# One product for router logits and actor outputs, and two channel attentions in the opening of a four-layer kernel

## The reference

```
x = x + channel_attention(layernorm(x))      # A
x = x + mixture_ffn(layernorm(x))            # F, weights shared by both F layers
x = x + attention_sps(layernorm(x))          # B
x = x + mixture_ffn(layernorm(x))            # F
```

```
probs  = softmax(h @ router_w.T)                          # 8 experts
a_h    = gelu(h @ actor_w1.T + actor_b1)                  # 50 hidden units
k      = argmax(clip(a_h @ actor_w2.T + actor_b2)) + 1    # 6 outputs
mask   = rank(probs) < k                                  # the k best experts
out    = sum_e where(mask, probs, 0)[e] * down_e(silu(gate_e(h)) * up_e(h))
```

## Time and profile before

| | |
|---|---|
| three runs | 488.0, 489.6, 489.79 us, median 489.6 |
| the profiled execution | 489.73 us |
| its span (first to last instruction) | 487.9 us |
| TensorE, VectorE, ScalarE, GpSimd busy | 98%, 62%, 55%, 64% |
| mean granted TensorE clock | 0.997 |

### The profile page before, as it was taken

One profiled execution on the slowest core, in us unless ns is written; L12 is line 12 of the kernel. 1 busy time (PEld: TensorE's weight loads), 2 busy tenths in 40 slices (PEclk: granted clock), 3 DMA queues, 4 the chain that ended last, 5 costly groups with the idle time before them and its releaser, 6 DMA issues.

```text
span 487.9 us, 6499 instructions
## 1 busy us (share of the span) xinstructions
PE 476.1 (98%) x2039; PEld 342.7 (70%) x2039; DVE 303.0 (62%) x718; ACT 266.2 (55%) x484; POOL 312.4 (64%) x326
## 2 busy tenths in 40 slices
PE   8899899999999999999999999999999999999997
PEld 7777666677676666666676766677676777778886
DVE  3656342646487768499836884359754565666563
ACT  3395636646724693348742649235772456456551
POOL 5355789336948576486463466467675586778774
PEclk9999899999999999999999999999999999999999
DMA  7700000000000000000000000000000000000000
GB/s 240 247 0 2 0 1 0 1 1 1 1 0 2 1 0 1 1 1 1 0 1 0 1 2 0 1 1 5 19 0 2 0 23 1 0 1 10 15 0 22
DMA packets 7933, 7.36 MB, mean 15 GB/s; under 512 B 732, under 2 KB 7772, under 8 KB 7900
## 3 DMA queue, kind: packets, MB, share of 16 engines
q1 hardware_dynamic: 7900, 6.96, 4.4%
HBM read 5.91 MB, written 1.05 MB: 14 GB/s over the span
## 4 chain that ended last, share of the span: by engine, by line
PE 83%; ACT 2%; DVE 1%; POOL 1%; issue 0%; ACTq 0%; DVEq 0%; POOLq 0%
PE bank L1313 21%; PE bank L1128 17%; PE bank L1130 17%; PE bank L1129 17%; PE bank L1351 3%; PE bank L1249 1%; PE bank L1343 1%; PE bank L1151 1%; PE bank L1363 1%; PE bank L1321 1%; PE bank L1257 1%; PE bank L1291 1%; ACT L778 1%; PE bank L1239 0%; PE bank L1219 0%
## 5 line engine op out<-in xcount | busy, mean ns | idle before, releaser
L647 POOL TENSOR_TENSOR t<-t,sl 128x512 f32<-128x512 f32 x105 | 148.6, 1421 | 80.9 <-DVE t L1069 61.7
L778 ACT ACTIVATE sl<-bank 128x512 f32<-128x512 f32 x168 | 99.2, 596 | 126.3 <-PE bank L1130 114.5
L1313 PE MATMUL bank<-t,WD 128*128 128x512 f32 x256 | 126.0, 592 | 0.0
L1069 DVE TENSOR_TENSOR t<-bank,sbc 128x512 f32<-128x512 f32 x105 | 72.3, 689 | 72.2 <-PE bank L1130 70.5
L1128 PE MATMUL bank<-xhF,WGh 128*128 128x512 f32 x167 | 89.8, 538 | 1.0 <-ACT sl L778 0.9
L647 POOL TENSOR_TENSOR t<-t,sbc 128x512 f32<-128x512 f32 x63 | 79.4, 1288 | 0.2
L1069 DVE TENSOR_TENSOR t<-bank,sl 128x512 f32<-128x512 f32 x63 | 42.9, 686 | 55.8 <-ACT sl L778 30.0
L1128 PE MATMUL bank<-xhF,WUh 128*128 128x512 f32 x168 | 66.8, 397 | 1.1 <-DVE t L1069 1.1
L1130 PE MATMUL bank<-xhF,WUl 128*128 128x512 f32 x168 | 66.3, 395 | 0.0
L1129 PE MATMUL bank<-xlF,WUh 128*128 128x512 f32 x168 | 66.3, 394 | 0.0
L1130 PE MATMUL bank<-xhF,WGl 128*128 128x512 f32 x167 | 66.2, 397 | 0.0
(11 more groups left out here) (210 smaller groups left out, 722.9 us busy)
## 6 DMA issues: line engine op xcount, KB each, us to landing
stage<-in_gate SPq DMA_DIRECT2D x7, 192.0 KB, 5.7
stage<-in_up SPq DMA_DIRECT2D x7, 192.0 KB, 5.7
WD<-in_down SPq DMA_DIRECT2D x7, 192.0 KB, 5.7
X<-in_x SPq DMA_DIRECT2D x4, 256.0 KB, 5.4
out<-X SPq DMA_DIRECT2D x3, 256.0 KB, 2.3
raw<-in_small SPq DMA_DIRECT2D x1, 384.0 KB, 4.2
out<-X SPq DMA_DIRECT2D x2, 128.0 KB, 1.9
raw<-in_small SPq DMA_DIRECT2D x1, 192.0 KB, 2.7
```

What stands on the lines that cost most here:

```text
L647: pool.tensor_tensor(t2[k % NT2][:, :], t2[k % NT2][:, :], by[:, :], ALU.mult).then_inc(a_done, 1)
L778: act.activation(sl[k % NSL][:, :], bank[k % 2][:, :], ACT.Silu).then_inc(silu_done, 1)
L1069: dve.tensor_tensor(t2[k % NT2][:, :], bank[2 + k % 2][:, :], by[:, :], ALU.mult).then_inc(t2_done, 1)
L1313: r = pe.matmul(OACC[:, :], WD[:, c, :], t2[k % NT2][:, :], start=(c == 0), stop=(c == CH - 1 or k == TAIL[0] - 1))
```

## The change

Router: the second weight `w2` becomes 72 x 14: the actor's 50 x 6 and, at rows 64 to 71, an 8 x 8 identity in columns 6 to 13. "gelu" writes into rows 0 to 49 of `xa`, and "act" multiplies all 72 rows of `xa` by it, which gives actor outputs and router logits per token in one bank. The transposes of "rt" on TensorE and their turn are gone; the VectorE steps "rt", "rcmp", "rrank", "rmax" stand behind "act", and its bank is freed by "actk". The step lists of the feed-forwards follow, and that of the second starts earlier.

Opening: both of the first two batches go through channel attention in it, and `A1_STEPS` is gone. For these two, the raw tokens are transposed; the weights take up the norm weight and the centring (a product with a centred, scaled identity, "wn"); the Gram matrix is the raw tokens times tokens over variance, with a VectorE reciprocal for GpSimd's power; and the root is put on when "y" is added. Batch 0 needs no "am2": its values are made ahead ("vT"). Sums of squares are a step of their own ("asq"). An early idle Silu loads its table. The warming products are fewer and read zeros. SP loads the columns and batch 1 earlier, and waits for `w2`'s constants before `w2`. The head mask takes three GpSimd instructions.

```diff
-PRELUDE = [("stats", "A", 0), ("rstd", "A", 0), ("warm", 0), ("xn", "A", 0), ("ag", 0), ("xT", "A", 0), ("ar", 0), ("wph", 0), ("wph", 1),
-           ("warm", 1), ("asim", 0), ("ass", 0), ("apow", 0), ("wpl", 0), ("swh", 0), ("wv", 0), ("warm", 2), ("ascale", 0), ("asT", 0),
-           ("amax", 0), ("warm", 3), ("aexp", 0), ("awo", 0), ("am", 0), ("stats", "A", 1), ("rstd", "A", 1), ("wpl", 1), ("am2", 0),
-           ("y", 0), ("warm", 4), ("wp", 3), ("stats", "F", 0), ("rstd", "F", 0), ("xn", "A", 1), ("ag", 1), ("xn", "F", 0), ("wp", 4),
-           ("xT", "F", 0), ("xT", "A", 1), ("xl", "F", 0), ("ar", 1), ("swl", 0)]
-WARM = (12, 2, 4, 7, 10)
+PRELUDE = [("warm", 0), ("xT", "A", 0), ("warm", 1), ("stats", "A", 0), ("rstd", "A", 0), ("wn", 0), ("xn", "A", 0), ("ag", 0),
+           ("stats", "A", 1), ("rstd", "A", 1), ("xn", "A", 1), ("ar", 0), ("ag", 1), ("asq", 0), ("asim", 0), ("ass", 0), ("apow", 0),
+           ("wph", 0), ("wpl", 0), ("ar", 1), ("vT", 0), ("wph", 1), ("asq", 1), ("ascale", 0), ("ass", 1), ("apow", 1), ("asT", 0),
+           ("asim", 1), ("amax", 0), ("aexp", 0), ("warm", 2), ("ascale", 1), ("asT", 1), ("awo", 0), ("amax", 1), ("am", 0), ("aexp", 1),
+           ("wpl", 1), ("warm", 3), ("awo", 1), ("silu", 0), ("y", 0), ("am", 1), ("xT", "A", 1), ("wv", 0), ("swh", 0), ("am2", 1),
+           ("warm", 4), ("stats", "F", 0), ("rstd", "F", 0), ("xn", "F", 0), ("xT", "F", 0), ("xl", "F", 0), ("wp", 3), ("wp", 4),
+           ("y", 1), ("swl", 0)]
+WARM = (6, 5, 5, 4, 8)
...
-A1_STEPS = [(2, "asim"), (3, "ass"), (3, "apow"), (4, "ascale"), (7, "asT"), (7, "amax"), (8, "aexp"), (9, "awo"),
-            (11, "am"), (12, "am2"), (14, "y")]
-F0_STEPS = [(0, "route"), (1, "inner", 0), (1, "rt"), (2, "rcmp"), (2, "rexp"), (3, "inner", 1), (3, "rrank"), (3, "rmax"),
-            (4, "rsum"), (5, "tanh"), (6, "gelu"), (8, "act"), (8, "actk"), (9, "sx"), (11, "sbc")]
-F1_STEPS = [(0, "stats"), (0, "rstd"), (0, "xn"), (3, "xT"), (4, "xl"), (6, "route"), (7, "inner", 0), (8, "rt"), (9, "rcmp"), (9, "rexp"),
-            (9, "inner", 1), (10, "rrank"), (10, "rmax"), (11, "rsum"), (11, "tanh"), (12, "gelu"), (14, "act"),
-            (14, "actk"), (15, "sx"), (17, "sbc")]
+F0_STEPS = [(0, "route"), (1, "inner", 0), (2, "inner", 1), (3, "tanh"), (4, "gelu"), (5, "act"), (5, "rt"), (6, "rcmp"), (6, "rexp"),
+            (7, "rrank"), (7, "rmax"), (8, "rsum"), (8, "actk"), (9, "sx"), (10, "sbc")]
+F1_STEPS = [(5, "stats"), (6, "rstd"), (8, "xn"), (10, "xT"), (11, "xl"), (13, "route"), (14, "inner", 0), (15, "inner", 1), (16, "tanh"),
+            (17, "gelu"), (19, "act"), (19, "rt"), (20, "rcmp"), (20, "rexp"), (21, "rrank"), (21, "rmax"), (22, "rsum"),
+            (22, "actk"), (23, "sx"), (25, "sbc")]
...
-F_STEPS = [(0, "stats"), (1, "rstd"), (2, "xn"), (4, "xT"), (5, "xl"), (6, "route"), (7, "inner", 0), (8, "rt"), (9, "rcmp"), (9, "rexp"),
-           (10, "inner", 1), (10, "rrank"), (10, "rmax"), (11, "rsum"), (12, "tanh"), (13, "gelu"), (15, "act"),
-           (15, "actk"), (16, "sx"), (18, "sbc")]
+F_STEPS = [(0, "stats"), (1, "rstd"), (2, "xn"), (4, "xT"), (5, "xl"), (6, "route"), (7, "inner", 0), (9, "inner", 1), (10, "tanh"),
+           (11, "gelu"), (13, "act"), (13, "rt"), (14, "rcmp"), (14, "rexp"), (15, "rrank"), (15, "rmax"), (16, "rsum"),
+           (16, "actk"), (17, "sx"), (19, "sbc")]
...
+YT_FROM = (32, 53, 69, 87, 108, 130, 152)
...
-TURNS = dict(xT=1, wv=1, ag=1, ar=1, asim=1, asT=1, am=1, am2=1, y=1, route=1, rt=1, act=1, sbc=1, yT=1,
+TURNS = dict(xT=1, wv=1, ag=1, ar=1, asim=1, asT=1, am=1, am2=1, y=1, route=1, act=1, sbc=1, yT=1,
              bqk=1, bs=1, bpT=1, bo=1, bw=1, wbT=1, wqk=1, wvp=1, wa=1)
 
 
-FREED_BY = dict(asim="ascale", asT="amax", act="actk", rt="rmax")
+FREED_BY = dict(asim="ascale", asT="amax", act="actk")
...
-    threads += [[CH * (n + 1) + 3, [(0, ("yT", n))], 0] for n in range(2 * NB - 1)]
+    threads += [[max(CH * (n + 1) + 3, YT_FROM[n]), [(0, ("yT", n))], 0] for n in range(2 * NB - 1)]
     threads += [[M_START, [(0, ("wc", 0)), (2, ("wbT", 0)), (3, ("wqk", 0)), (4, ("wvp", 0)), (5, ("wa", 0))], 0]]
     threads += [thread("B", b, B_STEPS, B_STARTS[b]) for b in range(NB)]
-    threads += [thread("A", 1, A1_STEPS, 0)] + [thread("A", b, A_STEPS, A_STARTS[b - 2]) for b in range(2, NB)]
+    threads += [thread("A", b, A_STEPS, A_STARTS[b - 2]) for b in range(2, NB)]
...
-        w2 = sb("w2", [AH, KMAX + 2])
+        w2 = sb("w2", [R0 + E, KMAX + E])
...
+            sp.dma_start(cols[:, :], cols_d).then_inc(cols_loaded, 16)
             sp.dma_start(raw[:, 0:C_OUT], small_d[:, 0:C_OUT]).then_inc(qkv_loaded, 16)
-            sp.dma_start(cols[:, :], cols_d).then_inc(qkv_loaded, 16)
+            sp.dma_start(X[:, NT:2 * NT, :], xv[:, 1]).then_inc(x_loaded[1], 16)
             for j in range(2):
                 sp.dma_start(stage[j][:, :], (gate_d, up_d)[j][:, 0:WCOLS]).then_inc(stage_loaded[j], 16)
             sp.dma_start(raw[:, C_OUT:C_ALL], small_d[:, C_OUT:C_ALL]).then_inc(small_loaded, 16)
-            sp.dma_start(X[:, NT:2 * NT, :], xv[:, 1]).then_inc(x_loaded[1], 16)
             sp.dma_start(rows[:, :], rows_d.partition_broadcast(P)).then_inc(rows_loaded, 16)
-            sp.dma_start(w2[:, 0:KMAX], w2_d).then_inc(rows_loaded, 16)
+            sp.wait_ge(w2_ready, 1)
+            sp.dma_start(w2[0:AH, 0:KMAX], w2_d).then_inc(rows_loaded, 16)
...
-                    if b:
-                        wait_free(pool, turn_of["asT", b - 1])
+                    if b > 1:
+                        wait_free(pool, turn_of["asT", b - 2])
                     if b == 0:
                         pool.wait_ge(etemp_ready, 1)
-                    chain(pool.tensor_tensor(rs[:, :], ss[:, :], nhalf[:, 0:2], ALU.pow))
-                    pool.tensor_tensor(qn[:, :], rs[:, 1:2], etemp[:, 0:1], ALU.mult).then_inc(norms_ready, 1)
+                    chain(pool.tensor_tensor(rss[b % 2][:, :], ss[:, :], nhalf[:, 0:2], ALU.pow))
+                    pool.tensor_tensor(qns[b % 2][:, :], rss[b % 2][:, 1:2], etemp[:, 0:1], ALU.mult).then_inc(norms_ready, 1)
...
-            act.wait_ge(qkv_loaded, 32)
+            act.wait_ge(cols_loaded, 16)
             act.activation(etemp[:, :], cols[:, 5:6], ACT.Exp).then_inc(etemp_ready, 1)
+            act.wait_ge(ci_ready, 1)
+            act.activation(cenw[:, :], cenw[:, :], ACT.Identity, scale=cols[:, 0:1]).then_inc(cenw_ready, 1)
...
+                if kind == "wn":
+                    act.wait_ge(wn_full, 1)
+                    act.activation(raw[:, 0:C_OUT], bank[2][:, 0:C_OUT], ACT.Copy).then_inc(wn_ready, 1)
+                if kind == "vT":
+                    act.wait_ge(vT_full, 1)
+                    act.activation(YT[:, :], bank[0][:, :], ACT.Copy).then_inc(vT_ready, 1)
+                if kind == "silu":
+                    act.activation(junk[:, :], cols[:, 5:6], ACT.Silu)
...
+            dve.memset(sl[0][:, 0:P], 0.0).then_inc(zeros_ready, 1)
...
+            chain(dve.memset(w2[:, :], 0.0))
+            dve.wait_ge(consts_ready, 1)
+            dve.tensor_copy(w2[R0:R0 + E, KMAX:KMAX + E], ident[R0:R0 + E, R0:R0 + E]).then_inc(w2_ready, 1)
...
+            dve.wait_ge(consts_ready, 1)
+
+            dve.tensor_scalar(cenw[:, :], ident[:, :], 1.0 / D, None, ALU.subtract).then_inc(ci_ready, 1)
...
+                    if seq < 2:
+                        rinv = rinvs[seq]
+                        dve.wait_ge(stats_ready, seq + 1)
+                        chain(dve.tensor_scalar(rinv[:, :], mv[:, :, 1], 1.0 + RMS_EPS, RMS_EPS * LN_EPS, ALU.mult, ALU.add))
+                        chain(dve.reciprocal(rinv[:, :], rinv[:, :]))
...
+                    if seq < 2:
+
+                        for i in range(NT):
+                            dve.tensor_scalar(xn[:, i, :], X[:, NT * q + i, :], rinvs[seq][:, i:i + 1], None, ALU.mult).then_inc(xn_ready, 1)
+                        continue
+                    if seq == 2:
+                        wait_full(dve, turn_of["ag", 0])
...
-                            r = dve.tensor_tensor(X[:, i, :], bank[i][:, 0:P], X[:, i, :], ALU.add)
+                            if i == 0:
+                                dve.wait_ge(rstd_ready, 1)
+                            r = dve.scalar_tensor_tensor(X[:, i, :], bank[i][:, 0:P], rstds[0][:, i:i + 1], X[:, i, :], ALU.mult, ALU.add)
...
+                    if s == ("y", 1):
+                        dve.wait_ge(rstd_ready, 2)
+                        for i in range(NT):
+                            x_ = X[:, NT + i, :]
+                            r = dve.scalar_tensor_tensor(x_, m_bank(t)[:, i * P:i * P + P], rstds[1][:, i:i + 1], x_, ALU.mult, ALU.add)
+                        r.then_inc(n_free(t), 1)
+                        continue
...
-                    t = turn_of["rt", n]
-                    logits = m_bank(t)[:, 0:NT * E].rearrange("p (i e) -> p i e", e=E)
+                    t = turn_of["act", n]
```

(62 more changed lines are left out.)

87 lines of the change are left out of this document (44 added, 43 removed).

## The result

The changed kernel takes 501.1 us (median of four, 499.3 to 505.5); beside it the kernel before took 488.8. The ratio is 1.0268, with a 95% interval of 1.0218 to 1.0318: slower, where faster was forecast. The profiled execution was the longest of the four, 505.5 us with a span of 503.5, at a mean granted TensorE clock of 0.983; the other three had 0.993 to 0.997. Each later kernel is compared with runs of the kernel before on the same chip, whose median was 488.0 to 489.6 us.

The account below looks back on a forecast made before the run. Behind the opening TensorE was taken to bound the kernel. From 489.7 us, less 4.3 (transposes), 3.0 (72 rows), 2.2 (batch 1's attention), 4.0 (first-block stalls) and 0.7 (opening), it forecast 475.5 us, range 471 to 483.

Parts of the forecast that it names:

- The step that failed: Router: VectorE's ranking behind "act" holds one of three rotating banks until "actk"; under gate and up tiles this costs nothing.
- slower rival: Routers: the held bank makes TensorE wait; at 2.5 us a router it ends at 495.5 us; chance 0.06.
- Transposes out: Router: the four small "rt" transposes go eight times, 0.54 us a time, saving 4.3 us.
- 72 rows: Router's "act": contracting 72 rows instead of 50 takes 0.79 us instead of 1.17, saving 3.0 us over eight times.
- 72 rows drain as 50 do: Router's "act": 72 rows behave as 50 do, so the 3.0 us are missing, 478.5 us; chance 0.13.
- First block (-4.0): First routed block: waits on ScalarE and VectorE and the half clock, together 4.7 us, go; 4.0 us taken.
- first block stays as full of holes: First routed block: the second feed-forward's steps replace batch 1's on busy ScalarE; no 4.0 us gain, 479.5 us; chance 0.16.
- the prediction's own sign of being wrong: Changed profile: a half clock behind the opening would show the prediction wrong; no size given.
- its other sign: Changed profile: new TensorE waits on ScalarE in the first block or before each block's start would show it wrong.
- Opening (-0.7): Opening: of the 0.83 us of batch 0's removed second mixing 0.7 us is kept; the removed power's gain is eaten.
- the 2.2 us of batch 1: First block: TensorE steps of batch 1's attention move to the opening at no cost there, saving 2.2 us.
- The change doesn't do what it says: Router: the transposes' time returns as waits for the longer chain behind "act"; 483.5 us; chance 0.04.

Follow-up runs that it names:

- Kernel 1: Changed kernel, with the step that needs the bank held for the selection put at least one slot later by the planner: 489.4 us, ratio 1.0007 to the kernel before.
- Kernels 6: Changed kernel with VectorE's clamp of the actor's logits run five times instead of once: 509.0 us, ratio 1.0433 to the kernel before.
- 11: Changed kernel with the six selection steps that need only the actor's logits moved ahead, behind the copy of the logits: 497.1 us, ratio 1.0169.
- kernel 10: The change's router on the old opening, with later bank step, packed ranking and repacked first-block router: 488.4 us, ratio 0.9993 to the kernel before.
- 12: kernel 9 with the six selection steps that need only the actor's logits moved ahead, behind the copy of the logits: 483.4 us, ratio 0.989.
- kernel 5: Kernel 1 with the first block's tanh, gelu and joined product one slot later, the ranking packed behind: 488.4 us, ratio 0.9996 to the kernel before.
- kernel 8: The change's router alone on the old opening, with the step that needs the held bank one slot later: 490.2 us, ratio 1.0038 to the kernel before.
- kernel 9: Changed kernel with three edits of order: later bank step, packed ranking, repacked first-block router: 486.2 us, ratio 0.9954 to the kernel before.
- kernels 3: Changed kernel with the router of before, so the new opening alone: 488.9 us, ratio 1.0001 to the kernel before.
- kernel 2: Changed kernel with the joined product's bank given back at once; ranking and selection read an SBUF copy: 500.4 us, ratio 1.0242 to the kernel before.

## Why the prediction was wrong, by its own steps

**The step that failed** is "That costs nothing while gate and up tiles, which have banks of their own, cover it", with the sentence set against the slower rival, "the planner defers such steps rather than letting TensorE wait". The planner does defer, but to the slot in which the selection is issued, and it doesn't count how long VectorE then takes. At routers 2 to 6 the list has nothing between the selection and the TensorE step that needs the bank; at router 0 one tile lies between and is too short. Measured: six waits of 1.0 to 2.0 us, 10.6 us in all. Kernel 1, which removes 6.9 us of them by place alone, is 11.7 us faster; 2.9 us of that are waits for SiLU that go with its order. Kernels 6 and 11 show it from both sides: 0.9 us more chain, 0.9 us more wait; 1.3 us less chain, 1.2 to 1.4 us less wait where it had been longer than that. The mechanism was on the list as the slower rival, with its price too high (2.5 us, measured 1.0 to 2.0) and its chance of 0.06 far too low. In the kernel before the logits' bank was freed by the ranking's last step under the same rule; but there other steps and at least a gate and up tile came to lie between, so the trace showed no such wait, and I read that as a property of the planner.

**Transposes out:** right; the group is gone. With the 72-row product it should save TensorE 4.3 + 2.2 = 6.5 us by the sizes measured below; in kernel 10, on the old opening, TensorE is busy 468.8 us, 5.6 less than the 476.1 before without its 1.7 us of half clock.

**72 rows:** right in kind, mis-sized. The eight instructions took 0.80 us, not 0.68: 0.80 + 0.33 - 0.23 = 0.90 us, not 0.79, and 8 x (1.17 - 0.90) = 2.2 us for 3.0. The product behind it takes 0.33 us as behind the 128-row group (0.34), not 0.42; the rival "72 rows drain as 50 do" is out. The Trainium skill ("TensorEngine Tiling (Array Packing)", Key Properties) states that changing the tiling mode drains TensorE; the 0.33 us behind 72 rows and the 0.42 behind 50 agree with it, if 72 rows run in the mode of the neighbours.

**First block (-4.0):** the waits that it counted did go: the 1.9 us on the scales' copy and the half clock around 50 us. But the half clock was, by the clocks on record, there only in part of the executions: of the 68 executions of the kernel before beside kernels 1 to 12, 33 took 489.4 to 490.0 us at a granted clock of 0.997, as the profiled one did, and 31 took 487.8 to 488.1 at 1.000. What came is larger than what went. The new router is one chain, gelu, product, ranking, selection, `sx`, while before the ranking ran beside the gelu. TensorE waits 2.4 us for the gelu, 1.9 for `sel`, 1.1 for `sx`, and loses 3.4 us of clock: 8.8 us. The rival "first block stays as full of holes" named this, with another cause (ScalarE under the second feed-forward). In kernel 5, which starts the chain a slot later, 2.1 us of the gelu wait and the 1.9 for `sel` go, and the wait for `sx` at the chain's end grows by 2.6. Kernel 10 has the same chain, only packed ahead of other steps: 0.4 us of the gelu wait are left and none for `sx`, where kernel 8, on the same opening, had 3.1 and 1.9. So what stands between the chain's steps in the queues counts, and not its length alone. A half clock behind the opening was the prediction's own sign of being wrong, and it came; its other sign looked for new waits on ScalarE, and the large ones are for VectorE.

**Opening (-0.7):** nothing. The first gate product came no earlier, and the opening alone is no different from before. Of the 2.2 us of batch 1 nothing shows by itself either: they lie in the opening, which didn't get shorter, and the holes that closed in the first block were paid again by new ones (0.8 us on `SWl`, 1.74 us on SiLU at 182.67). In kernel 9 against kernel 10 the opening is worth some 2 us.

**"The change doesn't do what it says"** (0.04) holds in part: in kernels 8 and 10 the router saves TensorE time and the time is that of before, because waits took its place, for a longer chain in the main.

**The account:** 475.5 forecast; + 11.7 (what kernel 1's place in the list takes away), + 8.8 (first block), + 1.8 (the wait at router 3 that kernel 1 keeps), + 0.8 (joined product), + 0.7 (opening), + 0.8 (`SWl`) = 500.1, of 501.1. The first term is a difference of times, the others are read from rows, of executions at different clocks; that only 1.0 us is left may be chance.

**Not settled:** why the SiLU waits of 1 to 1.7 us arise in the later blocks of the changed kernel and of kernels 3, 11 and 12. The traces show what ScalarE did before them. In kernel 3 two table loads of 1.28 us each, for attention B's exponential and back, lie ahead of the late SiLU. In kernel 12 ScalarE had stood 3.82 us for GpSimd's step of the router:

```profile
176.53 0.63 ACT L779 ACTIVATE hq<-hq 50x512 f32<-50x512 f32 x1 [3.82 <-POOL hq L623]
```

The waits come with a new order of the same steps; no run varied them alone.

## What to carry to other kernels

Where a planner counts a buffer as free once its last reader is *listed*, look at what the next writer finds: the price is the reader's remaining chain minus the work in front of the writer on its own queue, and a merge that appends more work to that chain raises it at every turn. Two products in one save engine time, but they also put two chains that ran side by side into one; cost the new chain from its first input to its last reader, stage by stage, before counting the saving. A dose in both directions (a few idle steps more, a few steps moved ahead) tells in two runs whether a chain is what an engine waits for.

## What the runs showed of the hardware

VectorE's comparison of 128x256 took 0.42 us each time with the bank as operand, but 0.41 to 1.51 us with both inputs in SBUF (kernel 2). The reduction with one input took 0.42 us always. Two timelines of kernel 2, VectorE's and then GpSimd's:

```profile
202.24 1.51 DVE L1057 TENSOR_TENSOR scr<-lgs 128x256 f32<-128x256 f32 x1
...
205.84 0.41 DVE L1060 TENSOR_TENSOR scr<-scr,tri 128x256 f32<-128x256 f32 x1
206.28 1.37 DVE L1062 TENSOR_TENSOR scr<-scr,gt 128x256 f32<-128x256 f32 x1
```

```profile
202.07 1.40 POOL L650 TENSOR_TENSOR t<-t,sbc 128x512 f32<-128x512 f32 x1 [3.78 <-DVE t L1107]
206.00 1.38 POOL L650 TENSOR_TENSOR t<-t,sbc 128x512 f32<-128x512 f32 x1 [2.53 <-DVE t L1107]
```

The two long ones start while a GpSimd product runs and end 0.3 us behind it; the short one started 0.16 us before the next product did. Two of the reductions lie wholly inside a GpSimd product (at 328.78 and 438.70 us) and took 0.42 us all the same. The Trainium skill ("SBUF — State Buffer", Who interferes with whom) states that a VectorE instruction with two SBUF inputs contends with a GpSimd instruction that reads SBUF, and that a reduction doesn't; these rows agree.

A hole doesn't always lower the granted clock. Behind the 2.04 us wait at 199 us of the changed kernel it fell to 0.50; behind the 2.93 us wait at the same place with the dose it stayed at 1.00, by the same view:

```profile
201.00:203.00 2.00, 2.00 (x13) 1.80 (x14) 0.00 (x0) 1.25 (x3) 1.17 (x2) 1.00 0.00 0
203.00:205.00 2.00, 2.00 (x8) 1.31 (x7) 0.33 (x1) 1.55 (x3) 0.00 (x0) 1.00 0.00 0
```

Executions of one kernel differ in the same way. With the dose they took 506.6, 509.0 and 514.1 us at mean granted clocks of 0.990, 0.986 and 0.977; 0.013 x 510 = 6.6 us of lost clock, by my estimate, stand against the 7.5 us between the first and the last. So what a wait costs beyond its length isn't read from one profile.
